# A fourth key stack for the last attention of a four-stage kernel, laid over the dead float32 queries

## What is computed

```python
q = (query @ Wq.T + bq).reshape(B, Sq, H, Hd).transpose(0, 2, 1, 3)
k = (key @ Wk.T + bk).reshape(B, Skv, H, Hd).transpose(0, 2, 1, 3)
v = (value @ Wv.T + bv).reshape(B, Skv, H, Hd).transpose(0, 2, 1, 3)
scores = jnp.einsum('bhqd,bhkd->bhqk', q * SCALE, k)
attn = jax.nn.softmax(scores, axis=-1)
out = jnp.einsum('bhqk,bhkd->bhqd', attn, v).transpose(0, 2, 1, 3).reshape(B, Sq, D)
out = out @ Wo.T + bo
x = x + jnp.tanh(g_xattn[1]) * out
```

## Time and profile before

| | us |
|---|---|
| runs: lowest, median, highest of 3 | 566.93, 570.64, 570.78 |
| profiled execution | 572.05 |
| its span | 570.3 |
| mean granted clock of PE | 0.817 |
| busy: PE, DVE, ACT, POOL | 381.9, 389.9, 266.4, 84.8 |
| SP queue: MB moved, share of 16 DMA engines | 50.37, 37.1% |
| chain that ended last: PE, DVE, ACT, DMA | 39%, 33%, 13%, 6% |

### The profile page before, as it was taken

One profiled execution on the slowest core, in us unless ns is written; L12 is line 12 of the kernel. 1 busy time (PEld: TensorE's weight loads), 2 busy tenths in 40 slices (PEclk: granted clock), 3 DMA queues, 4 the chain that ended last, 5 costly groups with the idle time before them and its releaser, 6 DMA issues.

```text
span 570.3 us, 9305 instructions
## 1 busy us (share of the span) xinstructions
PE 381.9 (67%) x2998; PEld 255.8 (45%) x3002; DVE 389.9 (68%) x1644; ACT 266.4 (47%) x684; POOL 84.8 (15%) x215
## 2 busy tenths in 40 slices
PE   2899799812229699777898888899999404403006
PEld 2558586501127455553576666676455201103004
DVE  7643999989983759996876666671454574474773
ACT  3854544622231566245575565877443351452440
POOL 6791000000006063630420000000000000000000
PEclk9998699955558799989888899999999855855556
DMA  9800002377203588430694855501990000000002
GB/s 266 243 1 1 0 2 98 120 142 160 49 1 96 110 135 161 142 97 20 128 157 74 203 82 84 83 1 46 410 371 22 1 0 2 0 1 0 2 1 64
DMA packets 38534, 50.96 MB, mean 89 GB/s; under 512 B 5957, under 2 KB 35030, under 8 KB 37334
## 3 DMA queue, kind: packets, MB, share of 16 engines
q1 hardware_dynamic: 38486, 50.37, 37.1%
HBM read 40.28 MB, written 9.97 MB: 88 GB/s over the span
## 4 chain that ended last, share of the span: by engine, by line
PE 39%; DVE 33%; ACT 13%; DMA 6%; issue 5%; POOL 3%; SPq 1%; DVEq 0%; ACTq 0%; POOLq 0%
PE ps L2166 8%; ACT below L1759 7%; DVE PR L1057 5%; DMA ks<-key_parts 4%; PE ps L2000 4%; PE ps L2105 3%; PE ps L2116 3%; PE ps L2130 3%; DVE R L991 2%; PE ps L1945 2%; DVE prod L1053 2%; PE ps L1861 2%; ACT E L1727 2%; DVE PR L1055 2%; PE ps L2286 2%
## 5 line engine op out<-in xcount | busy, mean ns | idle before, releaser
L1271 DVE TENSOR_REDUCE negm<-ps 112x1 f32<-112x375 f32 x128 | 64.3, 542 | 28.6 <-PE ps L2105 28.2
L1727 ACT ACTIVATE E<-ps 125x448 f32<-125x448 f32 x96 | 49.3, 545 | 28.8 <-PE ps L2116 27.0
L2254 PE MATMUL ps<-cnt,same 128*128 128x7 bf16 (+3 forms) x36 | 6.2, 171 | 71.1 <-ACT below L1759 65.1
L2105 PE MATMUL ps<-ks,qs 96*112 96x375 bf16 x128 | 44.8, 365 | 9.9 <-DMA ks<-key_parts 6.8
L2116 PE MATMUL ps<-qs,ks 99*125 99x112 bf16 x384 | 40.1, 231 | 5.3 <-ACT E L1727 3.4
L2116 PEld LDWEIGHTS ps<-qs,ks 99*125 99x125 bf16 x384 | 35.8, 145 | 13.7 <-ACT E L1727 10.1
L1259 DVE TENSOR_REDUCE acts<-gel 128x4 f32<-128x448 f32 x32 | 19.8, 621 | 30.9 <-ACT gel L1691 30.9
L2254 PEld LDWEIGHTS ps<-cnt,same 128*128 128x128 bf16 (+1 forms) x36 | 4.0, 110 | 73.9 <-issue 73.9
L2130 PE MATMUL ps<-E,v 125*32 125x112 f32 x768 | 31.5, 274 | 0.1
L1691 ACT ACTIVATE gel<-ps 128x448 f32<-128x448 f32 x32 | 17.3, 543 | 29.3 <-PE ps L2166 29.3
L788 POOL CAST kp<-kx 128x750 bf16<-128x750 f32 x8 | 6.5, 812 | 163.2 <-ACT path L1605 125.1
(11 more groups left out here) (372 smaller groups left out, 1014.0 us busy)
## 6 DMA issues: line engine op xcount, KB each, us to landing
ks<-key_parts SPq DMA_DIRECT2D x48, 187.5 KB, 6.7
piwT<-fn_process_input_weights SPq DMA_DIRECT2D x4, 2048.0 KB, 16.9
key_parts<-kp SPq DMA_DIRECT2D x48, 93.8 KB
ctx_again<-in_ctx SPq DMA_DIRECT2D x7, 512.0 KB
keys<-kx SPq DMA_DIRECT2D x16, 187.5 KB, 2.1
kx<-keys SPq DMA_DIRECT2D x8, 375.0 KB, 6.0
ctxP<-in_ctx SPq DMA_DIRECT2D x8, 256.0 KB, 6.5
patT<-in_L_ffn_input_patterns SPq DMA_DIRECT2D x1, 2048.0 KB, 14.3
```

Source lines behind the costliest of these rows:

```text
L1271: drain(dve.tensor_reduce(negm[:, n:n + 1], bank(nm)[0:S, 0:SC], AX.X, ALU.max, negate=True), nm)
L1727: drain(fn(E[:, (KCH * f + c) % 6, :], bank(nm)[0:KC, 0:4 * S], ACT.Exp), nm)
L2105: fill(mm(bank(nm)[0:S, 0:SC], qs[0:SR, n, S * (u // 4):S * (u // 4) + S], ks[0:SR, u // 4 % 3, n, :], start=True, stop=True), nm)
```

## The change

`ks` keeps three stacks. A fourth, `ks_last`, is laid over `qx32` and the first part of `qp`, which are dead by then. Batch b uses place b % 4, through a small function `stack(b)`. The stack of batch 3 no longer waits for a place: SP fills it, and its rows of ones by a DMA of its own, right after the last load of the queries. The stacks of batches 4 to 7 wait for the batch four before, not three. There are four semaphores for loaded stacks, and one for the new ones.

```diff
         after_queries = rt.at
         qp = rt.take("qp", [128, 2, 3, TOK], BF16)
+        ks_last = Region(queries_at).take("ks_last", [128, NH, SC], BF16)
+        assert queries_at + 2 * NH * SC <= rt.at
+
+        def stack(b):
+
+            return ks_last[:, :, :] if b % 4 == 3 else ks[:, b % 4, :, :]
...
-        stack_loaded = [sem(f"stack_loaded{i}") for i in range(3)]
+        stack_loaded = [sem(f"stack_loaded{i}") for i in range(4)]
...
-                    sp.dma_start(ks[HD * j:HD * j + HD, b % 3, :, :], key_parts[b, part]).then_inc(stack_loaded[b % 3], 16)
+                    sp.dma_start(stack(b)[HD * j:HD * j + HD], key_parts[b, part]).then_inc(stack_loaded[b % 4], 16)
...
-            for b in range(3, B):
-                wait_filled(sp, ("scoreT", 4 * b - 9, KCH - 1))
+            sp.dma_start(stack(3)[SR:SR + 3], onesb[0:3, :].unsqueeze(1).broadcast_to([3, NH, SC])
+                         ).then_inc(loaded["ones_last"], 16)
+            load_stack(3)
+            for b in range(4, B):
+                wait_filled(sp, ("scoreT", 4 * b - 13, KCH - 1))
                 load_stack(b)
                 if b == 4:
                     sp.wait_ge(x_ready, 2 * B)
...
-                        pe.wait_ge(stack_loaded[u // 4 % 3], 16 * len(K_PARTS) * (u // 12 + 1))
+                        pe.wait_ge(stack_loaded[u // 4 % 4], 16 * len(K_PARTS) * (u // 16 + 1))
+                    if u == 12:
+                        pe.wait_ge(loaded["ones_last"], 16)
...
-                fill(mm(bank(nm)[0:S, 0:SC], qs[0:SR, n, S * (u // 4):S * (u // 4) + S], ks[0:SR, u // 4 % 3, n, :],
+                fill(mm(bank(nm)[0:S, 0:SC], qs[0:SR, n, S * (u // 4):S * (u // 4) + S], stack(u // 4)[0:SR, n, :],
...
-                             ks[0:SR + 3, f // 4 % 3, n, KC * c:KC * c + KC],
+                             stack(f // 4)[0:SR + 3, n, KC * c:KC * c + KC],
```

More of the change, by code:

```diff
@@ L477, in bankb @@
             return ps[plan[name].banks[0]][:, :].bitcast(BF16)
-        names = ("x",) + tuple(f"ctx{b}" for b in range(B)) + ("again", "ones_k", "attnW", "ffnW", "small", "biasT", "pat", "oiw",
+        names = ("x",) + tuple(f"ctx{b}" for b in range(B)) + ("again", "ones_k", "ones_last", "attnW", "ffnW", "small", "biasT", "pat", "oiw",
                  "opat", "pval", "piw")
@@ L618, in _ @@
             for b in range(3):
-                sp.dma_start(ks[SR:SR + 3, b, :, :], onesb[0:3, :].unsqueeze(1).broadcast_to([3, NH, SC])
+                sp.dma_start(stack(b)[SR:SR + 3], onesb[0:3, :].unsqueeze(1).broadcast_to([3, NH, SC])
                              ).then_inc(loaded["ones_k"], 16)
```

## The result

| | before | after |
|---|---|---|
| median of 20 runs, us | 571.66 | 567.9 |
| lowest, highest | 566.93, 577.93 | 563.1, 574.6 |
| profiled execution, its span | 572.05, 570.3 | 563.1, 561.4 |
| granted clock of PE, mean | 0.817 | 0.83 |

The ratio after to before is 0.9924, 95% interval 0.9901 to 0.9946: some 4.3 us faster, where 10.2 was forecast (560.4, range 555.5 to 565). The profiled execution happens to be the fastest of the 20, and 8.95 us faster than that of before. Read alone, it says that the forecast nearly came true. Three more traces of the same kernel say something else. The ratio leaves out the slow executions, those more than 1.5% above the fastest of their kernel, so it is a little lower than that of the two medians in the table.

A forecast was written before the change was run, and what follows sets the result against it. PE was taken to set the pace, held up by late key stacks and the slow clock behind the holes. 10.36 us saved less 0.2 for stack 3 gave 10.2, from 570.64 to 560.4 us; range 555.5 to 565.

The forecast's parts named there:

- (c): Steps opening with a new stack: VectorE's maxima come with 0.44 us left, nothing replaces the holes, cost 0.
- (a): Batches 4 to 7: stacks issued four steps earlier, three holes and the slow clock behind them go, 10.36 us saved.
- (b): Stack 3, issued right behind the queries: lands net 0.2 us later, so step 7 keeps its 2.3 us hole.
- R1: Rival: PE's low clock comes as often at other small waits, only the holes go, 7.3 us saved, 563.3; chance 0.13.
- R2: Rival: stack 3 comes in time too, step 7 loses hole and slow step, 14.2 us saved, 556.4; chance 0.13.
- R3: Rival: stack 3 shares the DMA engines with stack 4 and patT and lands late, 2.2 us slower, 572.9; chance 0.03.
- R4: Rival: the hole labelled "issue" at step 11 is not a load and stays, 6.2 us saved, 564.4; chance 0.06.
- the case that I gave 0.06: The whole kernel's time within 1% of before; chance 0.06.

The follow-up runs named there:

- order_deep: Changed kernel with stack 3, half the second queries, stack 4, the other half in this order, patT behind stack 7, all issued at once: ratio to before 0.9895.
- order_shallow: Changed kernel with stack 3, half the second queries, stack 4, the other half, patT last, at most three of these loads under way: ratio to before 0.983.
- traffic: Kernel before, with DRAM-to-DRAM copies of stacks 3 to 7 added behind their loads, nothing waiting for them: ratio to before 1.0001.
- before_pat_late: Kernel before, with patT issued behind the load of batch 7 instead of batch 4: ratio to before 1.001.
- hold4: Changed kernel, with stack 4 and patT held back until behind step 6 instead of step 3: ratio to before 0.994.
- the last version: Changed kernel with stack 3, half the second queries, stack 4, the other half, patT last, at most four loads under way: 563.01 us, ratio to before 0.9807.

## Why the prediction was wrong

The measured 567.9 us lies above the end of the range, 565, and the gain is 4.3 us where 10.2 were forecast.

- **The step that failed is (c), "what is late next", with the sentence "Nothing takes the place of the holes there".** I asked which data would be late, found VectorE's maxima with 0.44 us to spare, and never asked for PE's instructions. One step behind the place where the load's hole at step 11 had been, the block for 12.2 is late in three of four traces. Steps 12 and 13 then take 12.1, 11.9 and 12.5 us in place of 5.8: 6.1 to 6.8 us more, on average over the four traces some 4.9. The hole is 3.6 to 4.1 us of that, the rest is the low clock behind it (in the third trace the granted clock is 0.50 from 328.1 to 334.1). No rival named it. The runs that move patT and that limit the loads under way show the cause. The same loads in the same order, at the same mean rate, make the blocks late when all are issued at once (order_deep) and not with three under way (order_shallow), so it is the backlog. Whether copies between places in DRAM would do the same stays open (traffic).
- **(a) was right in mechanism.** The holes at steps 11, 15 and 19 went in all four traces, and stacks 4 to 7 were never late there. Its 10.36 us needed that nothing else was late. The first step with a new stack came out 0.26 us longer than 3.23: ScalarE's exponential, which used to catch up in the hole, frees its bank later (the step's second product of line 2128 stands 0.80 us behind its opening, 0.59 before). That is 0.8 us for three steps. I had argued from busy shares that it holds the rate.
- **(b) had the landing right and the wait wrong.** Step 7 opened at 306.11, within 0.3 us of before, as forecast. But I reckoned the hole from one trace in which PE arrived at 304.2, behind a slow stretch. From the opening of step 3 to that of step 7 it is 13.8 and 15.4 us in the two traces of before (292.63 to 306.42 in the first), and 17.2, 14.7, 16.0 and 16.1 in the four after, about 1.4 us more (1.1 if the three-stack variants traffic and before_pat_late, 15.1 and 15.4, are counted in; and in the third trace of the changed kernel 3.14 us of it is a late block): before, the load hangs on PE's own step 3; now on the queries' queue, and an earlier PE waits longer.
- Together 4.9 + 0.8 + 1.4 are 7.1 of 10.2, which leaves 3.1; measured 4.3. The traces are few and the clock varies, so I take this as agreement, no more. The four traced executions also lean to the slow side: they took 0.985, 0.991, 1.001 and 1.000 of the median of before on their chips, 0.994 on average where the runs have 0.9924.
- **R1** (only the low clock moves) does not hold: in the 33.5 us without a hole it stayed high, and where it came between steps 7 and 20, in any of the traces, PE stood in a hole as it fell or had left one at most 1.6 us before. **R2** was half tried: stack 3 in time alone brings nothing, since PE then runs dry. **R3** fell with hold4. **R4** fell: the hole at step 11, labelled issue in the trace of before, went with the load, so the label does not tell a late load from late instructions. In these traces the place does: at the opening product of a step it was the load, in mid-step the block.
- The chances were wrong as well. 0.92 for faster by over 1% rested on one trace of before; the measured 0.76% lies in the case that I gave 0.06.

## What to carry to other kernels

Before counting a removed wait as gain, look at what arrives during it: here blocks of the engine's own instructions, on a queue of their own, whose lateness the holes had covered. Here, the more loads were issued ahead, the later the instruction blocks came; a ring one place deeper paid in full only with stacks 3 and 4 moved forward between the loads of the queries and a limit on how many loads are under way, and bulk that nobody waits for (patT) belonged behind those that somebody does. No run gives the three-stack kernel that order and limit, so how much of the last version's gain needs the fourth stack is not shown. Take more than one trace of each kernel when the median and the profiled run disagree.

## What the runs showed of the hardware that I had not expected

- PE's instructions come in packets of 16 KB on queue 8, one for about 2.7 steps (8 us) here, and from the start of a packet to PE's next instruction, when PE stands waiting for it, it took 3.1 to 3.5 us (about 2.4 past step 20).
- With up to 19 loads of 112 to 188 KB under way such a packet starts up to 2.1 steps later than with three, and up to 8.6 us later after PE's passage of the place before (order_deep, order_shallow). The Trainium skill describes the DMA engines as taking turns between queue rows packet by packet (DMA: Bandwidth & Descriptors, "Queues, rings and completion order"); by that rule alone a long backlog in one queue would delay the other by a packet. A single transfer of a key load (12,000 bytes) takes 1.3 to 1.4 us here; how many of them make one of the page's packets no run here shows, so it stays open whether the rule gives the delay. The measured one decides.
- With three loads of 188 KB under way the queries and stack 4 still land in time, stack 5 is 2.8 us late; the DMA share falls from 0.90 to 0.68 (order_deep and order_shallow, 284 to 330 us) at 124 and 123 GB/s. The queue's depth bought no rate in that stretch.
